# Splitting the normalised activations: the high part by a second affine step on the scalar engine, the low part in two halves on the vector engine

## The reference

```
h = _layernorm(x, axis=-1) * (1 + ca) + sa
x = x + ga * _L0_attn_ref(h, ...)
h = _layernorm(x, axis=-1) * (1 + cb) + sb
x = x + gb * _L0_ffn_ref(h, ...)
```

## Time and profile before

| | before |
|---|---|
| time, median of 3 runs | 1808.55 us (1806.81 to 1810.52) |
| profiled execution: its time | 1810.02 us |
| profiled execution: span of the core | 1808.2 us |
| PE busy | 1787.4 us (99%) |
| DVE busy | 1498.7 us (83%) |
| ACT busy | 745.8 us (41%) |
| POOL busy | 290.2 us (16%) |

### The profile page before, as it was taken

How to read it: one execution, slowest core, us unless ns; L and a number is a source line. 1 busy time by engine, 2 the same in 40 slices (tenths; PEclk the granted TensorE clock), 3 DMA queues, 4 the chain that set the end, 5 groups by cost and what they waited for, 6 DMA issues and landing times.

```text
span 1808.2 us, 45563 instructions
## 1 busy us (share of the span) xinstructions
PE 1787.4 (99%) x19149; PEld 1610.9 (89%) x19149; DVE 1498.7 (83%) x3483; ACT 745.8 (41%) x1433; POOL 290.2 (16%) x243
## 2 busy tenths in 40 slices
PE   8999999999999999999999999998999999999999
PEld 7799989999999989999999989987898988889898
DVE  6898888888888889888888888899778787877875
ACT  4333433334333344333333343344445445454553
POOL 1000000000000000000000000002243443434343
PEclk9999999999999999999999999999999999999999
DMA  6102001100001000210001000020211112121110
GB/s 233 37 21 76 25 26 48 44 29 25 25 25 47 26 25 25 83 37 25 25 25 45 29 25 25 25 71 24 94 47 70 59 59 71 47 71 53 65 59 35
DMA packets 44339, 86.29 MB, mean 48 GB/s; under 512 B 2388, under 2 KB 4200, under 8 KB 44136
## 3 DMA queue, kind: packets, MB, share of 16 engines
q1 hardware_dynamic: 44120, 83.38, 13.3%
q10 hardware_dynamic: 16, 0.00, 0.0%
HBM read 48.77 MB, written 34.60 MB: 46 GB/s over the span
## 4 chain that ended last, share of the span: by engine, by line
PE 94%; DVE 4%; issue 1%; ACT 1%; POOL 0%; DVEq 0%; ACTq 0%
PE bank L1285 64%; PE lvl L1285 9%; PE bank L1293 3%; PE bank L1401 3%; PE bank L1394 3%; PE bank L1393 3%; PE lvl L1362 3%; PE bank L1323 2%; PE bank L1385 1%; PE lvl L1345 1%; PE lvl L1380 1%; PE lvl L1374 1%; PE bank L1626 0%; DVE xk L948 0%; PE bank L1619 0%
## 5 line engine op out<-in xcount | busy, mean ns | idle before, releaser
L132 POOL TENSOR_TENSOR ln_rs<-ln_ve,mhalf 128x2 f32<-128x2 f32 x64 | 82.8, 1293 | 925.8 <-DVE ln_ve L127 925.8
L1285 PE MATMUL bank<-hT_hi,wq_hi 128*128 128x256 f32 x512 | 148.5, 290 | 1.2 <-DVE hT_lo L713 1.2
L1285 PE MATMUL bank<-hT_hi,wk_hi 128*128 128x256 f32 x512 | 148.2, 289 | 0.0
L1285 PE MATMUL bank<-xk_hi,fk_hi 128*128 128x256 f32 x512 | 145.1, 283 | 1.2 <-DVE xk_lo L961 1.2
L1285 PE MATMUL bank<-hT_lo,wq_hi 128*128 128x256 f32 x512 | 145.6, 284 | 0.0
L1285 PE MATMUL bank<-hT_hi,wq_lo 128*128 128x256 f32 x512 | 145.5, 284 | 0.0
L1285 PE MATMUL bank<-hT_lo,wk_hi 128*128 128x256 f32 x512 | 144.9, 283 | 0.0
L1285 PE MATMUL bank<-xk_lo,fk_hi 128*128 128x256 f32 x512 | 144.9, 283 | 0.0
L1285 PE MATMUL bank<-xk_hi,fk_lo 128*128 128x256 f32 x512 | 144.9, 283 | 0.0
L1285 PE MATMUL bank<-hT_hi,wk_lo 128*128 128x256 f32 x512 | 144.7, 283 | 0.0
L973 DVE TENSOR_TENSOR ka_lo<-rl,ka_hi 128x512 fp32r<-128x512 f32 x64 | 42.0, 698 | 112.4 <-ACT ka_hi L545 112.4
(11 more groups left out here) (230 smaller groups left out, 5674.0 us busy)
## 6 DMA issues: line engine op xcount, KB each, us to landing
xs<-in_L_attn_x SPq DMA_DIRECT2D x32, 512.0 KB, 3.7
x_scratch<-xs SPq DMA_DIRECT2D x32, 512.0 KB, 2.8
xs<-x_scratch SPq DMA_DIRECT2D x32, 512.0 KB, 3.5
out<-xs SPq DMA_DIRECT2D x31, 512.0 KB, 2.8
mod_raw<-in_L_wmod SPq DMA_DIRECT2D x6, 1024.0 KB, 8.2
raw_q<-in_L_attn_wq SPq DMA_DIRECT2D x2, 512.0 KB, 5.1
raw_k<-in_L_attn_wk SPq DMA_DIRECT2D x1, 1024.0 KB, 6.0
raw_v<-in_L_attn_wv SPq DMA_DIRECT2D x1, 1024.0 KB, 6.6
```

Of the source, the lines that this page charges most:

```text
L132: pool.tensor_tensor(out=ln["rs"][:, :], in0=ln["ve"][:, :], in1=mhalf[:, :], op=ALU.pow).then_inc(ln["rstd"], 1)
L1285: last = pe.matmul(dst, lhs(a, s), rhs(b, s), start=(t == 0), stop=(t == len(terms) - 1))
```

## The change

For every block but the first, ACT computes the affine step twice from the same bank: once into `hF` in float32 and once into `hT_hi`, whose type makes it the rounded high part. DVE no longer casts. It makes the low part in two halves of 128 x 512, and each half waits for the two pieces of `hF` and the two of `hT_hi` that it reads. PE waits for the new semaphore `h_top` of the high parts where it waited for `h_full`.

```diff
@@ h_affine, scalar engine
                         act.activation(hF[:, k, :], src, ACT.Identity, scale=scl[0][:, n // BPB, k:k + 1],
                                        bias=sft[0][:, n // BPB, k:k + 1]).then_inc(h_full, 1)
+                        if n > 0:
+                            act.activation(hT[0][:, k, :], src, ACT.Identity, scale=scl[0][:, n // BPB, k:k + 1],
+                                           bias=sft[0][:, n // BPB, k:k + 1]).then_inc(h_top, 1)
@@ vector engine
-                def h_high(n):
-                    dve.wait_ge(h_full, 4 * (n + 1))
-                    dve.tensor_copy(hT[0][:, :, :], hF[:, :, :]).then_inc(h_hi, 1)
-                    dve.wait_ge(h_hi, n + 1)
-                    dve.tensor_tensor(out=hT[1][:, :, :], in0=hF[:, :, :], in1=hT[0][:, :, :].bitcast(F32),
-                                      op=ALU.subtract).then_inc(h_lo, 1)
+                def h_low_parts(n):
+                    for half in range(2):
+                        part = slice(2 * half, 2 * half + 2)
+                        dve.wait_ge(h_full, 4 * n + 2 * half + 2)
+                        dve.wait_ge(h_top, 4 * (n - 1) + 2 * half + 2)
+                        last = dve.tensor_tensor(out=hT[1][:, part, :], in0=hF[:, part, :], in1=hT[0][:, part, :].bitcast(F32),
+                                                 op=ALU.subtract)
+                    last.then_inc(h_lo, 1)
@@ tensor engine, attention_body (the same for the wait ahead of the second k rows)
                     if n > 0:
-                        pe.wait_ge(h_full, 4 * (n + 2))
+                        pe.wait_ge(h_top, 4 * (n + 1))
                         t2(n - 1, 1 - par, 0)
@@ tensor engine, ahead of the first body
-                pe.wait_ge(h_full, 8)
+                pe.wait_ge(h_top, 4)
                 for ch in range(NC):
                     gate_rows(ch)
```

More of the change, by code:

```diff
@@ L203, in blocks @@
         idle_set = sem(ctx, "idle_set")
+        h_top = sem(ctx, "h_top")
         wq_in, rv_half, x3_half = (sem(ctx, n) for n in ("wq_first_in", "rv_half", "x3_half"))
@@ L1104, in attention_body @@
                     if n + 2 < NB:
-                        h_high(n + 2)
+                        h_low_parts(n + 2)
                     diagonal(n + 1, 1 - par)
@@ L1267, in _ @@
                         dve.tensor_copy(twice[:, i, :].rearrange("p (n two m) -> p n two m", two=2, m=m)[:, :, j, :], first_half)
-                h_high(1)
+                h_low_parts(1)
                 first_update(0, 0)
```

## The result

| | before | after |
|---|---|---|
| time, median of 4 runs | 1809.21 us (1806.81 to 1810.52) | 1825.83 us (1823.47 to 1826.70) |
| ratio | | 1.0091, 95% interval 1.0079 to 1.0103 |
| profiled execution: its time, span | 1810.02, 1808.2 us | 1823.47, 1821.5 us |

The change makes the kernel 16.6 us slower; 13.8 were forecast (1822.4, range 1817 to 1830).

The account below looks back on a forecast made before the run. PE, busy 99% of the span, was taken to bound the kernel through its handover from DVE's `og`. 29 bodies x 0.46 = 13.3 us plus 0.5 at the start gave 13.8, from 1808.55 to 1822.4 us, range 1817 to 1830.

Parts of the forecast that it names:

- sum of 13.8 us: Whole kernel: 13.3 us from 29 bodies plus 0.5 us at the start, added to the median of 1808.55.
- PE is the bound, and the `og` handover has 0.02 to 0.03 us of slack: Steady body: PE never stops; its fifth transpose loads 0.14 us behind `og`, and the handover itself takes 0.12.
- the 0.05 that a wait returns: PE's transposes of `og`: after a wait they start closer together, fifth load to q load 0.39 us instead of 0.44.
- ACT: four more steps at 0.454 us, hidden in themselves: ACT in each block: the added steps take 1.82 us, the eighth ends at 504.15, and ACT has the room.
- The rival with steps of 0.564: ACT's added steps do not overlap, PE is 0.90 us later per body, total 1836 us; chance 0.06.
- the estimate from the Trainium skill: ACT's price by the skill's budget: 0.51 us a step, 2.05 for four, sum some 21 us (1829).
- DVE: the second half starts 0.03 us behind the eighth step, the diagonal 0.60 later, 0.54 us later than before: DVE in each body: second half at 504.18, diagonal at 504.78 instead of 504.23, delaying the queued `xs` and `og`.
- PE is 0.46 us later in each body: PE's fifth load of the `og` transposes: 506.91 instead of 506.39, 0.51 us, less 0.05 returned by closer transposes.
- 29 bodies: The count of bodies with the repeated delay: bodies 0 to 29 without body 0, 29 x 0.46 = 13.3 us.
- The start: 0.5 us: Ahead of body 0 PE loses 0.3 us, at its end about 0.2; range of both 0.1 to 1.2.
- The signs: Expected in the trace: ACT's eight steps 3.75 us, DVE's second wait 1.2, fifth load 0.9 behind first, DVE busy 20 less.
- The rival "faster" or "same": Faster through DVE's 0.67 us less per block, chance 0.02; same within 0.2% if ACT's step is below 0.37 us, chance 0.07.

Follow-up runs that it names:

- dose_small: The kernel before with one extra 128 x 128 copy on DVE between the split and the diagonal, in 27 bodies; 1811.18 us, ratio 1.0011.
- act_only: The kernel before with four added ACT affine steps per block into an unread spare tile, PE waiting for them; 1808.40 us, ratio 0.9999.
- half_later: The changed kernel with the low part's second half moved on DVE behind diagonal, merge and `xs` update, just ahead of `og`; 1809.17 us, ratio 1.0003.
- one_wait: The changed kernel with each half of the low part waiting for `h_top` alone, without the `h_full` wait; 1824.27 us, ratio 1.0085.
- f_then_top: The changed kernel with ACT writing all four pieces of `hF`, then all four of `hT_hi`, instead of alternating; 1826.85 us, ratio 1.0099.
- before_again: The kernel before, unchanged, run once more for a second trace; its span was 1807.1 us.

## Why the prediction was right

It named the right mechanism, DVE's wait for ACT's eighth step with `og` queued behind it, and its sum of 13.8 us came out at 16.6. The mis-sized term is the delay of DVE's second half, because of the handover to it. By its steps:

- *PE is the bound, and the `og` handover has 0.02 to 0.03 us of slack.* Right: dose_small put 0.14 us there, and a body grew by 0.07, so that 0.02 are left as slack besides the 0.05 that a wait returns.
- *ACT: four more steps at 0.454 us, hidden in themselves.* Right: the run of eight takes 3.76 us (3.75 predicted) and act_only shows that it costs nothing. The rival with steps of 0.564 is out. So is the estimate from the Trainium skill (ScalarE: Activation LUTs, Rules for kernel authors): 0.51 us for a step would have made the total 21 us; the rows show 0.45 from start to start. Its advice to keep additions and multiplications on VectorE would have given the right answer here, but not for a reason of price: half_later and act_only leave all of the added work on ACT and lose nothing.
- *DVE: the second half starts 0.03 us behind the eighth step, the diagonal 0.60 later, 0.54 us later than before.* This is the mis-sized term. Between ACT's end and the half lie 507.81 - 507.71 = 0.10 us, the next start is 0.61 behind, and the diagonal is 0.64 us later (4.47 behind ACT's first step; before, 504.23 - 500.40 = 3.83). I had taken the handover from the cast, which waits for one semaphore; the half waits for two. one_wait measured the difference at 0.07. The other 0.03 are 0.01 each from ACT's run of eight, from the half's length and from my rounding down.
- *PE is 0.46 us later in each body.* It is 37.90 - 37.33 = 0.57. Of the 0.11 between the two, 0.10 are the step above; `og` follows the diagonal by 1.35 us instead of 1.34. Counted from ACT's first step, the fifth load comes after 510.56 - 503.95 = 6.61 us instead of 506.39 - 500.40 = 5.99, 0.62 later, and less the 0.05 that a wait returns this is 0.57. The 0.05 came as predicted: fifth load to q 0.39 us.
- *29 bodies.* Right. In the changed kernel there are 1227.90 - 126.18 = 1101.7 us from the first load of body 1 to that of body 30, in the kernel before 1213.48 - 128.30 = 1085.2. The difference is 16.5, or 0.57 in each of 29; f_then_top, with 1101.8, has the same.

```profile
126.18 0.42 PEld L1329 LDWEIGHTS bank<-ident,og 128*128 128x128 f32 x4
...
1227.90 0.42 PEld L1329 LDWEIGHTS bank<-ident,og 128*128 128x128 f32 x4 [0.18 <-ACT h L454]
```

```profile
128.30 0.53 PEld L1323 LDWEIGHTS bank<-ident,og 128*128 128x128 f32 x5
...
1213.48 0.42 PEld L1323 LDWEIGHTS bank<-ident,og 128*128 128x128 f32 x4 [0.19 <-ACT h L450]
```

- *The start: 0.5 us.* Right, where the clock at the start is alike. f_then_top and the first profile of before both have a granted clock of 0.77 from 40 to 55 us, and the first load of body 1 is at 128.64 and 128.30, 0.3 us apart. half_later and before_again both have 0.89, and it is at 128.86 and 128.32, 0.5 us apart. This is what half_later still loses in its trace.

```profile
128.64 0.42 PEld L1330 LDWEIGHTS bank<-ident,og 128*128 128x128 f32 x4
```

In the profiled execution of the changed kernel this load came at 126.18, 2.1 us earlier than before, with the clock at 1.00 from 40 to 55 us; one_wait, also with 1.00, has 126.07. That and a crossing without a slow stretch (from the first load of body 30 to that of the step behind it 37.8 us, 38.9 before) is why its span rose by only 13.3. With the clocks alike in both places, f_then_top against the first profile of before, the spans are 1825.2 and 1808.2 us, 17.0 apart: 16.6 in the bodies and 0.3 at the start.
- *The signs.* The eight steps, the wait between the halves (1.13 us, about 33 in total, where 1.2 and 35 were foretold) and PE's idle time behind `og` (11.5, foretold around 10) came as foretold, and the fifth load is 1.00 us behind the first where 0.9 was said. DVE's busy time fell by 16.9 us and not by 20: two halves are busy for 0.69 us each, the whole piece was for 1.23. The 20 counted from start to start.
- *The rival "faster" or "same".* DVE was freed of 16.9 us and nothing came of it, as half_later shows: with the loss taken away, the time is that of before, 1809.17 us beside 1808.71.

## What to carry to other kernels

Moving work from a busy engine to an idle one is no gain if the busy one then has to wait for it in the middle of its queue: what counts is the time of the last handover, and what is queued behind the wait. Before such a move, look at the instructions behind it on the waiting engine up to the next one that the bounding engine needs, and put those that don't depend on the result ahead of the wait; here that brought the time back to within 0.5 us of the kernel before, but not below it. A matrix engine that is 99% busy can still be one handover away from a loss in every body, and the distance is read from the starts of its weight loads, not from its idle time.

## What the runs showed of the hardware

- A vector instruction with two waits for another engine started 0.10 us behind the later event, with one wait 0.03 us. Dropping the one that the other implies is worth 0.07 us each time it is on the path.
- Two affine steps in a row from the same piece of a PSUM bank into different tiles follow each other as quickly as steps on different pieces: 0.45 us from start to start (504.42 - 503.95 = 0.47, and eight in 3.76).
- A single body was longer in the changed kernel and in f_then_top, 38.24 instead of 37.90 us, at the same place (the 22nd). In the changed kernel ACT's eighth step ended there at 883.91 + 0.60 = 884.51, and DVE's half started at 884.96, 0.45 us behind it instead of 0.10. Another was longer in the kernel before (37.54, the 27th, the one of the earlier trace rows). The cause of neither was looked for, and both stay open.
